# Attention stage: both query halves of a unit accumulated together, and one copy a unit out of the accumulator instead of two

## What is computed

```python
H, DK = 16, 16                                   # 16 heads of 16 channels, D = 256
qkv = (x @ w_qkv).reshape(b, n, 3, H, DK)        # b = 4, n = 1024 tokens
attn = jnp.einsum('bhnd,bhmd->bhnm', q, k) * (1.0 / np.sqrt(DK))
attn = jax.nn.softmax(attn, axis=-1)
y = jnp.einsum('bhnm,bhmd->bhnd', attn, v)
return y.transpose(0, 2, 1, 3).reshape(b, n, d) @ w_proj
```

## Time and profile before

| | us |
|---|---|
| median of three runs | 1548.32 |
| lowest and highest run | 1542.98, 1559.46 |
| the profiled execution, its own time | 1548.32 |
| its span in the trace | 1546.6 |

### The profile page before, as it was taken

How to read it: one execution, slowest core, us unless ns; L and a number is a source line. 1 busy time by engine, 2 the same in 40 slices (tenths; PEclk the granted TensorE clock), 3 DMA queues, 4 the chain that set the end, 5 groups by cost and what they waited for, 6 DMA issues and landing times. The chain is left out here.

```text
span 1546.6 us, 32157 instructions
## 1 busy us (share of the span) xinstructions
PE 1447.8 (94%) x11962; PEld 897.2 (58%) x11962; DVE 1265.9 (82%) x2433; ACT 1020.0 (66%) x1737; POOL 370.1 (24%) x633
## 2 busy tenths in 40 slices
PE   7688989998999999999999999999997779999997
PEld 7465656555655344444444444444444659999996
DVE  6899999964566689999999999999962867777773
ACT  3699999963433478888888888888885532222221
POOL 3011111103111012222222222222222732222222
PEclk9799999999999789999999999999998989999999
DMA  3300101014975634334444443344332775656561
GB/s 116 95 8 15 47 28 41 15 63 170 287 257 197 153 66 96 94 93 99 99 91 91 96 91 92 85 87 92 77 92 73 239 289 187 221 191 223 190 217 49
DMA packets 147307, 186.04 MB, mean 120 GB/s; under 512 B 68288, under 2 KB 99008, under 8 KB 147152
## 3 DMA queue, kind: packets, MB, share of 16 engines
q1 hardware_dynamic: 126896, 157.27, 35.2%
q0 software_dynamic: 19280, 26.46, 5.6%
q10 hardware_dynamic: 976, 0.24, 0.1%
HBM read 129.67 MB, written 54.21 MB: 119 GB/s over the span
## 5 line engine op out<-in xcount | busy, mean ns | idle before, releaser
L1685 ACT ACTIVATE at_p<-at_pst 128x512 f32<-128x512 f32 x1024 | 556.0, 597 | 91.2 <-PE at_pst L1735 79.5
L1699 DVE TENSOR_REDUCE at_mx<-at_pmx 128x2 f32<-128x1024 f32 x488 | 578.9, 1217 | 21.6 <-PE at_pmx L1726 16.3
L1747 PE MATMUL at_pacc<-at_p,at_v 128*32 128x256 f32 x4096 | 334.4, 399 | 0.4 <-ACT at_p L1685 0.2
L1726 PE MATMUL at_pmx<-at_k,at_q 48*128 48x512 f32 x976 | 249.7, 507 | 4.3 <-PEq L1204 2.0
L1735 PE MATMUL at_pst<-at_q,at_k 50*128 50x512 f32 x1024 | 219.6, 413 | 0.2 <-ACT at_p L1685 0.2
L1726 PEld LDWEIGHTS at_pmx<-at_k,at_q 48*128 48x128 f32 x976 | 92.5, 186 | 213.3 <-issue 142.8
L878 PE MATMUL ws_pA<-ident,ws_A 128*128 128x128 f32 x1088 | 149.9, 283 | 24.7 <-ACT ws_A L660 22.0
L878 PEld LDWEIGHTS ws_pA<-ident,ws_A 128*128 128x128 f32 x1088 | 119.9, 144 | 84.6 <-ACT ws_A L660 39.7
L1735 PEld LDWEIGHTS at_pst<-at_q,at_k 50*128 50x128 f32 x1024 | 157.5, 190 | 12.6 <-ACT at_p L1685 6.0
L1747 PEld LDWEIGHTS at_pacc<-at_p,at_v 128*32 128x32 f32 x4096 | 81.4, 109 | 137.6 <-ACT at_p L1685 78.8
L2250 DVE STREAM_TRANSPOSE ex_zr<-ex_row 32x64 f32<-32x64 f32 x608 | 143.1, 235 | 15.9 <-DMA ex_row<-scratch_routed 8.0
(11 more groups left out here) (269 smaller groups left out, 1612.5 us busy)
## 6 DMA issues: line engine op xcount, KB each, us to landing
ex_w<-in_L_ffn_w SPq DMA_DIRECT2D x39, 1024.0 KB, 5.7
at_q<-scratch_qs SPq DMA_DIRECT2D x192, 64.0 KB, 3.1
at_k<-scratch_ks SPq DMA_DIRECT2D x192, 64.0 KB, 3.2
ex_row<-scratch_routed SPq DMA_DIRECT2D x39, 258.0 KB, 5.0
scratch_qs<-gp_split SPq DMA_DIRECT2D x16, 512.0 KB, 4.0
scratch_ks<-gp_split SPq DMA_DIRECT2D x16, 512.0 KB, 4.5
scratch_v<-gp_v SPq DMA_DIRECT2D x8, 1024.0 KB, 6.0
at_v<-scratch_v SPq DMA_DIRECT2D x32, 256.0 KB, 3.8
```

The source lines that it names most:

```text
L1685: a.activation(pt[:, n % BUFS, k % 2, :], pst[(w * 2 * STEPS + k) % BANKS][:], ACT.Exp).then_inc(exped, 1)
L1699: v.reduce_max(mx[w % 2][:].rearrange("p (h n) k -> p h n k", h=2)[:, :, j // 2, j % 2], pmx[n % SLOTS][:], AX.X).then_inc(taken, 1)
L1726: last = nc.tensor.matmul(pmx[n % SLOTS][:, h, :], att.rows(qst[u], h, ROWS)[:, nt * P:(nt + 1) * P], att.rows(kst[u], h, ROWS)[:, kh * HA ...
L1747: last = nc.tensor.matmul(pacc[at:at + 2 * DK, p * QUARTER:(p + 1) * QUARTER], vst[u][:, t, h, :], pt[:, n % BUFS, h, c * QUARTER:(c + 1) ...
```

## The change

`s` is now split the other way round, in `scores` and in `values`: the key tile is the outer loop and the half alternates. Both halves of `pacc` are therefore open at once during the whole unit. The `values` of step 0 is left out, and that of step 1 does both halves in one: its matmuls write 512 columns each and carry the `start` flag for both halves. The other fourteen write 256 columns as before. `out` copies all 512 columns of `pacc` once a unit, behind the exp k = 4 of the next unit, and the `values` of step 1 waits for that copy. `fold` waits for one count a unit in place of two.

```diff
 def fold(self, sp, w):
-        sp.wait_ge(self.oed, 2 * (w + 1))
+        sp.wait_ge(self.oed, w + 1)
...
-    COPIES = 18, 2
+    COPY = 4
...
-            def out(w, p):
-                a.wait_ge(pv, w * STEPS + (p + 1) * BT)
-                if p == 0 and w >= 2:
+            def out(w):
+                a.wait_ge(pv, (w + 1) * STEPS)
+                if w >= 2:
                     a.wait_ge(outputs.y_out[w % 2], w // 2 * outputs.MOVES)
-                at = p * QUARTER
-                a.copy(oe[w % 2][:, at:at + QUARTER], pacc[:, at:at + QUARTER]).then_inc(oed, 1)
+                a.copy(oe[w % 2][:], pacc[:]).then_inc(oed, 1)
...
-                    if k == COPIES[0]:
-                        out(w, 0)
-                    if k == COPIES[1] and w:
-                        out(w - 1, 1)
-            out(UNITS - 1, 1)
+                    if k == COPY and w:
+                        out(w - 1)
+            out(UNITS - 1)
...
             def scores(n, h):
-                u, p, t = w % RING, s // BT, s % BT
+                u, t, p = w % RING, s // 2, s % 2
...
             def values(n):
-                u, p, t = w % RING, s // BT, s % BT
+                u, t, p = w % RING, s // 2, s % 2
+                if s == 0:
+                    return
+                first = 0 if s == 1 else p
                 pe.wait_ge(exped, 2 * n + 2)
-                if n and t == 0:
-                    pe.wait_ge(oed, 2 * w + p)
+                if s == 1 and w:
+                    pe.wait_ge(oed, w)
                 for h in range(2):
                     for c in range(2):
                         at = (2 * h + c) * 2 * DK
-                        last = nc.tensor.matmul(pacc[at:at + 2 * DK, p * QUARTER:(p + 1) * QUARTER], vst[u][:, t, h, :],
-                                                pt[:, n % BUFS, h, c * QUARTER:(c + 1) * QUARTER], start=(t == 0), stop=(t == BT - 1))
-                last.then_inc(pv, 1)
+                        out = pacc[at:at + 2 * DK, first * QUARTER:(p + 1) * QUARTER].rearrange("d (p j) -> d p j", j=QUARTER)
+                        last = nc.tensor.matmul(out, vst[u][:, t, h, :], pt[:, n % BUFS - p + first:n % BUFS + 1, h, c * QUARTER:(c + 1) * QUARTER],
+                                                start=(s == 1), stop=(s == STEPS - 1))
+                last.then_inc(pv, 2 if s == 1 else 1)
```

## The result

The changed kernel takes 1552.08 us (median of 20 runs, 1548.59 to 1570.87), the kernel before 1542.99 us (median of 20, 1538.57 to 1559.46). The ratio is 1.0055, with a 95% interval of 1.0034 to 1.0077: about 8.5 us slower (9.1 as the difference of the medians). I had forecast 1562.0 against 1548.32, 13.7 us slower, and had thought "within 1%" the likeliest. The time lies in the range. The loss is certain, but only some six tenths of what the sum said. Of the runs behind this document, three that fell into a slower state of the whole program are left out of the ratios and of all figures on low time.

A forecast was written before the change was run, and what follows sets the result against it. TensorE was taken to pace the attention stage; 30 x 0.46 = 13.8 us lost, 0.3 saved in units 0 and 1, the last copy 0.21 later, total +13.7 on 1548.32: 1562.0 us, range 1547 to 1574.

The forecast's parts named there:

- What bounds the kernel: Attention stage: TensorE paces at the place of the new copy, and VectorE waits for it at a unit's start.
- Fewer, larger copies: ScalarE, 32 copies of 512 columns for 64 of 256: saves 0.04 us a unit on an idling engine, worth nothing.
- The 0.72 us: Length of the 512-column copy by the Trainium skill's rule, against 0.585 from the trace; would make the time about 1566.
- The merged group: Step 1's values on TensorE: 1.00 us against 1.14 for two old groups, saving 0.14 us a unit if nothing waits.
- The new wait: TensorE's step 3: step 1's values wait for the copy behind exp k = 4, making step 4's scores 0.46 us later.
- Nothing gives it back: Rest of the unit: VectorE and ScalarE shift too, nothing runs faster than 1.24 us a step, so 0.46 us stays.
- VectorE's slack: Rival in the attention stage: VectorE paces and TensorE's 0.46 us vanishes, time 1548; chance 0.10.
- step-9 stall: About 0.1 us of TensorE near step 9, from VectorE's backlog after inversion and tops; expected to return unchanged.
- The fold: Goes out 1.45 us later, inversion 0.46 later; 1.3 us to spare, hidden at the median landing, not the longest (5.8).
- The rival: Fold lands too late, so VectorE and TensorE stand 0.9 us in units with loads; priced at 1572, chance 0.15.
- the term for units 0 and 1: Start of the attention stage: the two units save 2 x 0.14 = 0.3 us, with no loss in unit 1.
- The term for units 2 to 31: The wait for the copy in each of these units: 30 x 0.46 = 13.8 us.

The follow-up runs named there:

- the changed kernel again: The changed kernel, unchanged, run for a second trace: 1555.0 us, ratio 1.0049 to the kernel before.
- filled: Six 128-column matmuls of no use added on TensorE ahead of the attention stage; side by side, kernel before 1542.63 us, changed kernel 1557.46 us.

## Why the prediction was right about the unit and wrong about the sum

*What bounds the kernel.* Right. TensorE paces the unit's start, VectorE stood 0.69 us there, and a copy 0.48 later made the unit 0.49 longer.

*Fewer, larger copies, worth nothing.* Right: the copy took 580 ns (585 from the earlier trace rows). The new copies start 0.99 behind step 2's scores (1.04 forecast) and end at 1.57 (1.62). The 0.72 us, an estimate from the Trainium skill's "ScalarE: Activation LUTs", section "Rules for kernel authors", are too long for this copy, and so were the 4 us more in the time; that row of the page is for an ACTIVATE whose bias is a pointer operand, and this copy has no bias.

*The merged group.* Right in its length: 1.00 us, read off at the low clock in the earlier trace rows with its share of columns doubled.

*The new wait.* Right: values start 1.71 behind step 2's scores (1.67 forecast), step 4's scores 3.05 (3.00), a unit 0.49 to 0.51 longer (0.46).

*Nothing gives it back.* Right within the stage at full clock, but for its end: unit 30, whose second half has no maxima, is only 0.2 us longer (18.65 and 18.87 from scores to scores of step 2). VectorE's slack didn't absorb it, the step-9 stall stayed at 1.33. My account of that stall, though, with inversion and tops adding up, was wrong.

*The fold.* Right. What VectorE's inversions waited for in the changed kernel (us in all, times):

```profile
  DMA at_den<-at_oe: 13.8, 1
```

The one wait is in unit 31, where VectorE has nothing else to do. In units 1 to 30 the landing came first, mostly by the 1.2 to 1.3 us worked out and never by less than 0.6. The rival isn't wholly absent: in two other traces (the changed kernel again, and filled) one landing took 5.1 us, and that one unit was 0.1 us longer.

*The sum.* Here it failed. The step that failed is the term for units 0 and 1: I took their low clock from one trace as given and changed only 0.28 us there ("Units 0 and 1 save 2 x 0.14 = 0.3", and "I count no loss" for unit 1). Three things in it were wrong.

First, the low clock is no constant. The stretch runs from 7 to 44 us in the traces, and from the table it costs from under 1 us to 13.5 at 38; over the whole program, low time is by its medians 12 us shorter in the changed kernel, worth -4.9 us. Second, unit 0 saves nothing: 21.3 us with and without the change once the low clock is gone. Third, unit 1 isn't free, since the wait for the copy is there too: it takes 20.5 us against 20.0 wherever the low stretch has ended before it.

The term for units 2 to 31 was right. From the scores of step 2 in unit 2 to the end of the last copy, four traces of the changed kernel (one filled) take 616.3 to 616.8 us, four of the kernel before (two filled) 601.4 to 603.2: 14.1 between their middles, where 13.8 + 0.2 were forecast. With 0.5 for unit 1 the units cost 14.6, and 14.6 - 4.9 = 9.7 is 0.6 above the difference of the medians and 1.2 above the 8.5 of the ratio.

It is shown that the whole price is there when the low clock is equal or absent at the stage's start (12.4 to 12.8 us at equal low time, 14.8 directly), and that the length of the low stretch moves the time by as much as was missing. It is likely that unit 0's order shortens it. How a left-out group and a merged one do that, while TensorE is busy throughout in either, stays open, and so do the 2 us between 12.4 to 12.8 and 14.6.

*The base.* The same oversight moved the absolute time: 1562.0 was forecast and 1552.08 measured, of which 5.3 us are the base and 4.6 the difference. The profiled execution of before had 38 us of low clock at this place and 1548.32 us, and I added to that; the median of 20 runs was 5.3 us lower. I said that the profiled execution was also the median, which three runs couldn't bear out.

*The chances.* 0.56 for "within 1%" fits 0.55%. But the whole interval lies above 1, so calling it a tie would be wrong too; the forecast of a loss was the right part of it.

## What to carry to other kernels

Here an instruction order that left a hole on the pacing engine wasn't paid for by a cheaper group behind it: when work is left out of one step and the next waits for another engine, count from the event that releases it, and everything behind it shifts one to one (a copy 0.48 us later made the unit 0.49 longer). Merging two accumulations into one group binds its start to the later of the inputs and its copy to the whole bank; here that cost 0.5 us to save an estimated 0.14.

Before adding microseconds to one profiled execution, look at the granted clock behind each change of stage and how it varies between executions. A few matmuls of no use in a wait of TensorE that exists anyway can be worth as much as the change under study: 0.3 to 0.5% on the kernel before, for six matmuls that delay nothing. On the changed kernel, whose low stretch was mostly short already, they gained nothing that could be seen. So measure it on the kernel that is to be kept.

## What the runs showed of the hardware that I had not expected

- An idle stretch of 2.01 us on TensorE at a change of stages was followed by a granted clock of 0.5 in all thirteen traces without the filling, from 0.4 to 2.3 us after the matmuls resumed; with the stretch filled to 0.47 us it didn't fall there in three traces.
- At that low clock TensorE was busy throughout, and yet it stayed there for anything from 7 to 44 us, the kernel before for 14 in one execution and 38 in another.
- The cost of the low clock is 0.41 us for each us between runs, not 0.5; of a step at the start of attention, 0.32 of 1.24 us doesn't scale with it, an estimate from 2.16 and 1.24 us. The first 7 us at the start of the stage cost less than 1 us in all.
